# The output projection of a vision-transformer block as ten products over 128 rows

## What is computed

```python
h = tokens(x) @ W + b                       # and cls_tok in front
q, k, v = (n @ Wq.T), (n @ Wk.T), (n @ Wv.T)    # n = layernorm(h), 6 heads of 32
scores = q @ k^T * 32**-0.5 + lam * (q . anchor_h)
a = softmax(scores) @ v                     # heads side by side again: 197 x 192
h = h + a @ Wo.T                            # the output projection
h = h + ffn(layernorm(h))                   # 8-bit activations and weights, with bias
```

## Time and profile before

| | |
|---|---|
| time, median of 3 runs | 1877.42 us (1877.11 to 1879.56) |
| the profiled execution: time, span | 1878.18 us, 1876.3 us |
| mean granted TensorE clock | 0.981 |
| TensorE matmuls busy | 1782.4 us (95%), 16944 of them |
| weight loads busy | 1660.7 us (89%) |
| VectorE busy | 1441.3 us (77%) |
| ScalarE busy | 811.5 us (43%) |
| GpSimd busy | 731.0 us (39%) |
| the twelve output products of a turn (L785 to L787) | 253 to 254 ns each by the records, 130 us busy for each of the three lines |
| product into att (L1077) | 128 of 557 ns |
| a_lo (L1017) | 128 of 552 ns |

### The profile page before, as it was taken

How to read it: one execution, slowest core, us unless ns; L and a number is a source line. 1 busy time by engine, 2 the same in 40 slices (tenths; PEclk the granted TensorE clock), 3 DMA queues, 4 the chain that set the end, 5 groups by cost and what they waited for, 6 DMA issues and landing times.

```text
span 1876.3 us, 55378 instructions
## 1 busy us (share of the span) xinstructions
PE 1782.4 (95%) x16944; PEld 1660.7 (89%) x16944; DVE 1441.3 (77%) x3708; ACT 811.5 (43%) x1942; POOL 731.0 (39%) x1909
## 2 busy tenths in 40 slices
PE   1999999994999999999999999999999999999996
PEld 1999999994899999999999999999999999999984
DVE  4888888884677777777777777777777777777773
ACT  2000000001555555555555555555555555555552
POOL 3343453451243343343343343333333333333343
PEclk8999999997999999999999999999999999999996
DMA  9799999963444444444444444444444444444440
GB/s 278 190 301 302 317 293 294 311 218 118 139 130 140 130 126 140 130 126 139 131 125 140 131 125 140 132 124 138 133 123 140 133 123 140 132 124 139 134 119 24
DMA packets 214767, 303.42 MB, mean 162 GB/s; under 512 B 47584, under 2 KB 203635, under 8 KB 204612
## 3 DMA queue, kind: packets, MB, share of 16 engines
q1 hardware_dynamic: 204542, 227.27, 42.2%
q10 hardware_dynamic: 6054, 38.54, 7.2%
q0 software_dynamic: 4128, 37.06, 5.1%
HBM read 126.49 MB, written 58.29 MB: 98 GB/s over the span
## 4 chain that ended last, share of the span: by engine, by line
PE 72%; issue 1%; POOL 1%; DVE 1%; DMA 1%; SPq 1%; ACT 0%; POOLq 0%; DVEq 0%
PE o_bank L825 15%; PE bank L765 13%; PE bank L809 9%; PE bank L797 8%; PE bank L774 6%; PE bank L748 5%; PE o_bank L835 4%; PE o_bank L748 3%; PE bank L785 2%; PE bank L786 2%; PE bank L787 2%; PE bank L871 2%; PE o_bank L938 1%; SPq L684 0%; DMA k_st<-k_lo 0%
## 5 line engine op out<-in xcount | busy, mean ns | idle before, releaser
L1023 DVE TENSOR_REDUCE neg_max<-bank 99x2 f32<-99x394 f32 x768 | 418.7, 558 | 208.2 <-PE bank L797 207.9
L954 ACT ACTIVATE probs<-bank 99x396 f32<-99x396 f32 x768 | 384.9, 501 | 298.5 <-PE bank L809 298.1
L303 PE MATMUL bank<-e_t,xt 128*128 128x192 f32 x2352 | 387.9, 329 | 40.6 <-DVE xt L389 22.0
L303 PEld LDWEIGHTS bank<-e_t,xt 128*128 128x128 f32 x2352 | 386.3, 192 | 41.8 <-DVE xt L389 23.1
L825 PE MATMUL o_bank<-probs,vals 99*64 99x198 f32 (+1 forms) x3072 | 288.9, 336 | 0.3 <-issue 0.2
L797 PE MATMUL bank<-k_st,q_st 96*99 96x198 f32 x1536 | 271.6, 272 | 15.6 <-DMA k_st<-k_lo 7.6
L809 PE MATMUL bank<-q_st,k_st 98*99 98x198 f32 x1536 | 280.5, 264 | 3.2 <-ACT probs L954 3.1
L825 PEld LDWEIGHTS o_bank<-probs,vals 99*64 99x64 f32 (+1 forms) x3072 | 210.0, 137 | 49.8 <-issue 0.9
L389 DVE STREAM_TRANSPOSE xt<-x_t 128x256 f32<-128x256 f32 x588 | 215.0, 416 | 44.0 <-PE bank L303 43.5
L948 ACT ACTIVATE x_hi<-bank 128x396 fp32r<-128x396 f32 x128 | 63.1, 493 | 396.8 <-PE bank L748 396.8
L809 PEld LDWEIGHTS bank<-q_st,k_st 98*99 98x99 f32 x1536 | 197.6, 166 | 41.6 <-issue 36.6
(11 more groups left out here) (123 smaller groups left out, 3943.3 us busy)
## 6 DMA issues: line engine op xcount, KB each, us to landing
q_st<-q_hi SPq DMA_DIRECT2D x256, 148.5 KB, 2.7
k_st<-k_hi SPq DMA_DIRECT2D x256, 148.5 KB, 2.7
x_t<-in_x_dram ACTq DMA_DIRECT2D x26, 1344.0 KB, 19.2
x_t<-in_x_dram SPq DMA_DIRECT2D x26, 1344.0 KB, 22.0
xn_in<-xn_scratch SPq DMA_DIRECT2D x128, 148.5 KB
q_st<-q_lo SPq DMA_DIRECT2D x128, 148.5 KB, 2.7
k_st<-k_lo SPq DMA_DIRECT2D x128, 148.5 KB, 2.6
h_in<-h_scratch SPq DMA_DIRECT2D x128, 148.5 KB
```

Source lines behind the costliest of these rows:

```text
L303: last = pe.matmul(token_bank(p)[:, 0:D], xt[:, p, c // 3, c % 3, :], e_t[:, row_kind(t), col, c // 3, c % 3, :], start=c == 0, stop=c == 5)
L954: nc.scalar.activation(probs[:, n.slot, h, :, :], wide(T_BANK, TC), ACT.Exp).then_inc(exp_done, 1)
L1023: nc.vector.tensor_reduce(out=neg_max[:, n.slot, :, h], in_=wide(S_BANK[h % 2], TC)[:, :, 0:NTOK], axis=AX_X, op=ALU.max, negate=True).the ...
```

## The change

`project_output` takes the form of `project_values`. Its weights become a fourth entry of `wa_hi`, `wa_lo` and `wb` (chunks of 128 and 64 rows, the latter written twice), and the tiles `wo_hi`, `wo_lo` and `wo_raw` go. On the activation side, att gets 256 columns: heads 0 to 5 and then heads 4 and 5 again, which VectorE writes with a second product; att's transposes give 128 rows in place of 96, a_hi is copied with 128 rows, and a_lo is made in two pieces, 128 and 64 rows. For each chunk of tokens there are five products in place of six. Where the changed kernel's lines are named below, they are those of its own file.

```diff
-        wa_hi = sb("wa_hi", [DA, 3, D], F32R)
-        wa_lo = sb("wa_lo", [DA, 3, D], F32R)
-        wb = sb("wb", [2 * DB, 3, D], F32R)
+        wa_hi = sb("wa_hi", [DA, 4, D], F32R)
+        wa_lo = sb("wa_lo", [DA, 4, D], F32R)
+        wb = sb("wb", [2 * DB, 4, D], F32R)
...
-        wo_hi = sb("wo_hi", [DC, 2, D], F32R)
-        wo_lo = sb("wo_lo", [DC, 2, D], F32R)
...
-            for i in (Q, K, V):
+            for i in (Q, K, V, O):
                 scale = {"scale": SCALE} if i == K else {}
                 for chunk, dst in enumerate((wa_hi, wb)):
                     high(w_raw[:, i, chunk, :], dst[:, i, :], w_high, **scale)
-            high(wo_raw[:], wo_hi[:], w_high)
...
                         if j == 10:
-                            low(wo_lo[:], wo_raw[:], wo_hi[:], O)
+                            low_weights(O)
...
-    att = tile("att", [TC, NS, 2, D])
-    a_hi = tile("a_hi", [DC, NS, 2, TP], F32R)
-    a_lo = tile("a_lo", [DC, NS, 2, TP], F32R)
+    att = tile("att", [TC, NS, 2, DA + 2 * DB])
+    a_hi = tile("a_hi", [DA, NS, 2, TP], F32R)
+    a_lo = tile("a_lo", [DA, NS, 2, TP], F32R)
...
                 for c in range(2):
-                    acc = bank[0:TC, c * D:(c + 1) * D]
-                    for ic in range(2):
-                        hi = a_hi[:, n.slot, ic, c * TC:(c + 1) * TC]
-                        lo = a_lo[:, n.slot, ic, c * TC:(c + 1) * TC]
-                        pe.matmul(acc, hi, wo_hi[:, ic, :], start=ic == 0, stop=False)
-                        pe.matmul(acc, hi, wo_lo[:, ic, :], start=False, stop=False)
-                        last = pe.matmul(acc, lo, wo_hi[:, ic, :], start=False, stop=ic == 1)
+                    tokens = slice(c * TC, (c + 1) * TC)
+                    xa_hi, xa_lo = a_hi[:, n.slot, 0, tokens], a_lo[:, n.slot, 0, tokens]
+                    pairs = ((wa_hi[:, O, :], xa_hi), (wa_lo[:, O, :], xa_hi), (wa_hi[:, O, :], xa_lo),
+                             (wb[:, O, :], a_hi[:, n.slot, 1, tokens]), (wb[0:DB, O, :], a_lo[0:DB, n.slot, 1, tokens]))
+                    for i, (weights, inputs) in enumerate(pairs):
+                        last = pe.matmul(bank[0:TC, c * D:(c + 1) * D], inputs, weights, start=i == 0,
+                                         stop=i == len(pairs) - 1)
...
-                    pe.wait_ge(norm_done, c.count(1, 1))
-                    turn(o_bank[:, 0, :], att, c, DC).then_inc(at_done, 1)
+                    pe.wait_ge(norm_done, c.count(2, 2))
+                    turn(o_bank[:, 0, :], att, c, DA).then_inc(at_done, 1)
...
-                    copy(a_hi[:, c.slot, :, :], wide(o_bank[:, 0, :], DC), ahi_done)
+                    copy(a_hi[:, c.slot, :, :], wide(o_bank[:, 0, :], DA), ahi_done)
...
-                    nc.vector.tensor_tensor(att[:, c.slot, :, :].rearrange("p c (h d) -> p c h d", h=H),
-                                            heads[:, :, :, 0:HD], inv.unsqueeze(3).broadcast_to([TC, 2, H, HD]),
-                                            ALU.mult).then_inc(norm_done, 1)
+                    for heads_in, at in (((0, H), 0), ((H - 2, H), D)):
+                        part = slice(heads_in[0], heads_in[1])
+                        many = heads_in[1] - heads_in[0]
+                        nc.vector.tensor_tensor(
+                            att[:, c.slot, :, at:at + many * HD].rearrange("p c (h d) -> p c h d", h=many),
+                            heads[:, :, part, 0:HD], inv[:, :, part].unsqueeze(3).broadcast_to([TC, 2, many, HD]),
+                            ALU.mult).then_inc(norm_done, 1)
...
-                    low_part(a_lo[:, c.slot, :, :], wide(o_bank[:, 0, :], DC), a_hi[:, c.slot, :, :], alo_done)
+                    for ic, rows_in in enumerate((DA, DB)):
+                        last = nc.vector.tensor_tensor(a_lo[0:rows_in, c.slot, ic, :], wide(o_bank[:, 0, :], rows_in)[:, ic, :],
+                                                       a_hi[0:rows_in, c.slot, ic, :].bitcast(F32), ALU.subtract)
+                    last.then_inc(alo_done, 1)
```

More of the change, by code:

```diff
@@ L138, in build_tokens @@
 def build_tokens(nc, s):
-    (ctx, tokens, sb, sem, banks, ident, wa_hi, wa_lo, wb, wb_rest, wo_hi, wo_lo, ffn_w_bf, ffn_bias, minus_half,
+    (ctx, tokens, sb, sem, banks, ident, wa_hi, wa_lo, wb, wb_rest, ffn_w_bf, ffn_bias, minus_half,
      h_dram, xn_dram, x_rows) = (
-        s[n] for n in ("ctx", "tokens", "sb", "sem", "banks", "ident", "wa_hi", "wa_lo", "wb", "wb_rest", "wo_hi",
-                       "wo_lo", "ffn_w_bf", "ffn_bias", "minus_half", "h_dram", "xn_dram", "x_rows"))
+        s[n] for n in ("ctx", "tokens", "sb", "sem", "banks", "ident", "wa_hi", "wa_lo", "wb", "wb_rest", "ffn_w_bf", "ffn_bias", "minus_half", "h_dram", "xn_dram", "x_rows"))
     h_t, xn_t, stats, ln = (s[n] for n in ("h_t", "xn_t", "stats", "ln"))
@@ L151, in build_tokens @@
     tok_bias = sb("tok_bias", [B, D], F32, tokens)
-    w_raw = sb("w_raw", [DA, 3, 2, D], F32, tokens)
-    wo_raw = sb("wo_raw", [DC, 2, D], F32, tokens)
+    w_raw = sb("w_raw", [DA, 4, 2, D], F32, tokens)
     ffn_raw = sb("ffn_raw", [DC, 2, D], I8, tokens)
@@ L265, in _ @@
             load_half_row(sp, 1, (0, 1), x_half[1])
-            for i, w in enumerate(("wq", "wk", "wv")):
+            for i, w in enumerate(("wq", "wk", "wv", "wo")):
                 load(w_raw[:, i, :, :], s[w], small_landed)
-            load(wo_raw[:], s["wo"], small_landed)
             load(ffn_raw[:].bitcast(mybir.dt.int32), s["ffn_w"].rearrange("(a p) n -> p a n", p=DC), small_landed)
@@ L488, in step @@
                         if j == 2:
-                            dve.wait_ge(w_high, 8)
+                            dve.wait_ge(w_high, 9)
                             low_weights(Q)
@@ L495, in step @@
                         if j == 10:
-                            low(wo_lo[:], wo_raw[:], wo_hi[:], O)
+                            low_weights(O)
                         if j == 12:
-                            nc.vector.tensor_copy(wb_rest[0:DB, :, :], wb[0:DB, :, :].bitcast(F32)).then_inc(prep, 1)
+                            nc.vector.tensor_copy(wb_rest[0:DB, :, :], wb[0:DB, 0:3, :].bitcast(F32)).then_inc(prep, 1)
                 if t.fixed and t.n == G - 1:
@@ L580, in build_attention @@
 def build_attention(nc, s):
-    (ctx, attention, sb, sem, banks, ident, wa_hi, wa_lo, wb, wb_rest, wo_hi, wo_lo, ffn_w_bf, ffn_bias, minus_half,
+    (ctx, attention, sb, sem, banks, ident, wa_hi, wa_lo, wb, wb_rest, ffn_w_bf, ffn_bias, minus_half,
      h_dram, xn_dram, out) = (
-        s[n] for n in ("ctx", "attention", "sb", "sem", "banks", "ident", "wa_hi", "wa_lo", "wb", "wb_rest", "wo_hi",
-                       "wo_lo", "ffn_w_bf", "ffn_bias", "minus_half", "h_dram", "xn_dram", "out"))
+        s[n] for n in ("ctx", "attention", "sb", "sem", "banks", "ident", "wa_hi", "wa_lo", "wb", "wb_rest", "ffn_w_bf", "ffn_bias", "minus_half", "h_dram", "xn_dram", "out"))
     h_t, xn_t, stats, ln, o_bank = (s[n] for n in ("h_t", "xn_t", "stats", "ln", "o_bank"))
@@ L818, in attend @@
                 if n.reuses(1):
-                    pe.wait_ge(norm_done, n.count(1, 0))
+                    pe.wait_ge(norm_done, n.count(2, 0))
                 for p in range(HP):
@@ L1185 @@
             a = _np.ascontiguousarray(a.transpose(0, 1, 3, 5, 4, 2, 6).reshape(128, GROUPS, 2, 3, D)[:, RAW_ORDER])
-        if name in ("L0_attn_Wq", "L0_attn_Wk", "L0_attn_Wv"):
+        if name in ("L0_attn_Wq", "L0_attn_Wk", "L0_attn_Wv", "L0_attn_Wo"):
             a = a.T
-            if name != "L0_attn_Wv":
+            if name in ("L0_attn_Wq", "L0_attn_Wk"):
                 a = a.reshape(D, HG, 2, HD).transpose(0, 2, 3, 1).reshape(D, D)
             a = _np.ascontiguousarray(_np.stack([a[0:DA], _np.concatenate([a[DA:D], a[DA:D]])], axis=1))
-        if name == "L0_attn_Wo":
-            a = _np.ascontiguousarray(a.T.reshape(2, DC, D).transpose(1, 0, 2))
         if a.dtype == _np.int8:
```

## The result

The changed kernel takes 1970.5 us (median of 4 runs, 1968.1 to 1973.6) against 1877.7 us (median of 4 runs of the kernel before): a ratio of 1.049 (95% interval 1.048 to 1.051). The direction was forecast, the size was not: 1889.9 us, with a range that ended at 1901. The profiled execution has a span of 1969.2 us, 92.9 more than before.

A forecast was written before the change was run, and what follows sets the result against it. Bound: VectorE's chain to att, which TensorE awaits, nearly equal to TensorE's own. Per turn -0.16 + 0.04 + 0.21 + 0.015 (or -0.12 + 0.21 + 0.015) = +0.105 us; 125 turns, +12.5 us, 1889.9 us; range 1880 to 1901.

The forecast's parts named there:

- V's projection is this very shape: Output projection: ten products at V's 0.09 us each in place of twelve, so TensorE does 0.18 us less before turn_back.
- the release: VectorE: h1 and reciprocal start earlier as turn_back ends earlier, gaining 0.16 us a turn, 0.12 in one of three.
- The prediction's own sign of being wrong: Wrong if att's loads show no more idle time, or the turn grows while h1 and reciprocal start as late as before.
- TensorE waits for att, not the other way round: Att's transposes wait for VectorE's att product every turn; loads before att would idle 44 us in all, against 9.2.
- The second product: VectorE's added product into att: 0.29 us, overlapping the first by 0.08, wholly on the path, +0.21 us a turn.
- The rule that I had cited against the overlap: VectorE's next instruction waits until the pipe is empty, so the second att product would cost the full 0.29 us.
- Att's loads of 128 columns: TensorE's att transposes: a load takes 142 ns, not 126; only the first is exposed, +0.015 us a turn.
- a_lo and GpSimd's slack of 0.04: a_lo in two pieces, +0.075 us, delays statistics; beyond GpSimd's 0.04 slack, 0.04 reaches the reciprocal in two turns of three.
- The rivals: TensorE bounds after all, 1847.4 us (4%); chains cancel, 1877 (11%); no release, 1905.5 (7%); no overlap of products, 1900 (6%).
- No release: Rival, 7%: something else holds h1 and reciprocal in place, so +0.225 us a turn, 28 us, 1905.5 us.

The follow-up runs named there:

- e1: Changed kernel with the fifth output product of each chunk over 128 rows, not 64, and a_lo one instruction: 1888.4 us, 1.0057 of the kernel before.
- e6: Changed kernel with the fifth output product over 96 rows in place of 64: 1891.6 us, 1.0056 of the kernel before.
- e7: Changed kernel with the fifth output product over 65 rows in place of 64: 1893.5 us, 1.0067 of the kernel before.
- e3: Changed kernel with the second chunk's 64-row product moved to its front, so both stand side by side: 1927.3 us, 1.027 of the kernel before.
- e11: Changed kernel with the fifth output product over 32 rows in place of 64: 1969.6 us, 1.048 of the kernel before.
- e8: Kernel before, with the fifth product of V's projection over 64 rows in place of 97: 1936.1 us, 1.030 of the kernel before.
- e4: Kernel before with only the second product into att added, its columns never read: 1906.5 us, 1.014 of the kernel before.
- e2: e1 with a_lo made in two pieces of 128 rows each: 1891.5 us, 1.0058 of the kernel before.

## Why the prediction was wrong

- **"V's projection is this very shape" is the step that failed.** It is not. V's fifth product runs over 97 rows (`wb_rest`, `x_lo[0:BIAS_LO + 1]`), the output's over 64 (`wb[0:DB]`). I put the price of the difference at nothing, and TensorE is held up by 0.34 us for each of two, 0.68 a turn, in place of the 0.18 it was to gain: shown by e1, e6 and e7 (gone with more rows), e3 (halved with one passage), e11 (the same at 32) and e8 (present in V's projection). A like passage stood in the kernel before, and I did not ask what it was. Behind attention's products, whose weights have 64 columns, the two scores take 0.36 us, elsewhere 0.19 (its chain in order of time):

```profile
1102.83 2.17 PE o_bank L825 x24
1105.00 0.36 PE bank L809 x2
...
1106.61 0.19 PE bank L809 x2
```

The Trainium skill, "TensorEngine Tiling (Array Packing)", section "Key Properties", says that changing the tiling mode drains TensorE; its list of configurations has 128, 64 and 32 rows. The trace fits this, in starts of 0.18, 0.26 and 0.17 us for 0.09, and in 65 rows counting as 128. The page gives no time for it, and that a plain product's rows alone bring on such a change is my reading of these runs.
- **Its share in the sum.** With the release lost as well (turn_back comes 0.50 later, not 0.18 earlier), the turn grew by 0.71 for a forecast 0.105: 0.50 + 0.20. The prediction's own sign of being wrong came true: the turn grew while h1 and the reciprocal started no earlier.
- **TensorE waits for att, not the other way round: right.** e4 costs its +0.197 in full; the loads before att were idle for 34.5 us there and in the changed kernel, 37.4 in e2, against 9.2 (44 forecast).
- **The second product: right.** 279 ns for 290, starting 0.08 before the first ends: +0.20 for +0.21. The rule that I had cited against the overlap does not decide it. The Trainium skill, "VectorE: DVE Perf Modes", section "The DRAIN you can't avoid", goes on to say that a next instruction that is not held starts earlier, which I had left out; with that the trace agrees.
- **Att's loads of 128 columns: right,** 142 ns, nothing more.
- **a_lo and GpSimd's slack of 0.04: right as far as it can be seen,** 0.025 a turn in e2's trace, for a forecast 0.04 in two turns of three.
- **The release: right where it can happen.** In e1 h1 and the reciprocal move up to their predecessors. The forecast was 0.15 us on average, and the start of the first product into att moved by 0.135. It was never tried alone.
- **The rest of the sum.** The kernels nearest to the one forecast, without the 64 rows, are e2, e6 and e7: ratios of 1.0056 to 1.0067, which is 1888.2 to 1890.3 on the time before, and turns 0.095 to 0.113 longer; forecast 1889.9 and 0.105.
- **The rivals** had no place for this. "No release" named its mechanism in part (something else holds h1) but gave 0.225 a turn.

## What to carry to other kernels

Before a set of matmuls is called "the same shape" as another, compare the rows of each one, the smallest above all: here 64 or 32 rows among products of more cost three late starts, and padding with rows that add zero, or something harmless, cost TensorE nothing. A busy share of 95% did not make TensorE the engine to relieve; the question is which instruction starts just behind another engine's end in every turn. What is put in front of it cost in full here (e4), even on an engine that is idle for a quarter of the time.

## What the runs showed of the hardware

- Products over 65, 96, 97 and 128 rows follow each other every 0.09 us (192 columns, 32-bit); 64 or 32 rows among them start 0.18 us behind the one before, and the next two 0.26 and 0.17 later. Two of 64 rows side by side start 0.17 apart, and the next two follow after 0.18 and 0.17, so the pair costs what one alone does.
- A copy within SBUF on VectorE (99 x 128, 32-bit) beside a GpSimd step on two SBUF operands ends 0.08 to 0.10 us after it, in 127 turns of 128: it takes 226 ns alone, up to 487 beside it. A reduction that moves the same numbers takes 275 ns at any time. The Trainium skill, "SBUF — State Buffer", section "Who interferes with whom", has both: copies can take a pair of ports that VectorE shares with GpSimd, under an exclusive lock, and reductions on this chip never do. The trace agrees.
- A delay of 0.67 us in TensorE's stream lengthened the turn by only 0.42, because the stretch from the transposes of the maxima to Q's first product became 0.23 shorter (e8).
